# A graph-and-experts kernel on one core: the turning of slot rows and the flag moved one tile back, one batch of statistics split, and GpSimd made to wait for a comparison

## The chip, the cores and the metric

The kernel runs on 1 core of one Trainium2 chip. The metric is device time in microseconds (us). Before the change the median of 3 runs is 608.58 us (606.66 to 609.39). The profile is of one execution.

## The reference

Two layers over 2,500 nodes of 512 features and 80,000 edges sorted by target:

```
edge_index = stack([src, dst])
x = x + gnn(layernorm(x), edge_index)      # h = x + segment_sum(x[src], dst); relu(h @ W1 + b1) @ W2 + b2
x = x + ffn(layernorm(x))                  # softmax gate, top 2 of 8 experts, gelu(x W1[e] + b1[e]) W2[e] + b2[e]
```

The change lies wholly in the first part of the graph layer.

## The kernel before, in words

Each engine has its own written-out order of instructions, and semaphores (`S["..."]`) tie the orders together. The nodes are cut into 20 tiles of 125 rows. `segment_sum` is moved behind the first matrix: z = layernorm(x) W1 is computed for each tile, and the edges are turned into a matrix of counts, 125 "windows" of 20 target nodes each; the counts are then multiplied with z in five groups of 25 windows.

The first 120 us hold two strands of work that share the engines.

**The tiles.** For tile t, ScalarE makes the normed rows (`normal_rows`, tile `xn`), TensorE turns them (`turn_normal`, issued inside `first_layer(t-1)`), ScalarE takes them out of PSUM as float16 (`normal_columns`, `xT_top`), VectorE takes the remainder (`low_columns`, `xT_rest`), and TensorE makes three products of eight matmuls each (`first_layer(t)`: top by high weights, then the turn of tile t+1, then top by low weights, then remainder by high weights). ScalarE writes `z_hi` and `z` (`split_z`), and GpSimd subtracts them (`low_parts`, tile `z_lo`). The means and deviations come from VectorE in batches of tiles (`statistics(b)`, then ScalarE's `roots(b)`, then VectorE's `scales(b)`): batch 4 is tiles 10 to 14, batch 5 tiles 15 to 19. The rows of x for batch 4 are loaded by the queue of SyncE, those of batch 5 by that of ScalarE, once tile 9 has been normed.

**The edges.** VectorE makes keys of the edges (`edge_keys`), SyncE writes them to memory as `edge_pairs`, and GpSimd gathers from there four pieces of slots per window by indirect DMA (`slot_rows`). VectorE compares each edge with the next one and the 255th next (`compare_edges(0)`, `compare_edges(1)`): that tells whether the edges are in order and none is too crowded. `close_rows` puts the nodes' own edges into the gathered rows and sums the flaws. TensorE adds the flaws over partitions (`flaw_sum`), VectorE makes the flag of it (`flag_i`), and the flag goes through memory into `range_row`, from where all engines read it and branch; with these inputs the branch is not taken. TensorE turns the slot rows (`turn_rows`, two parts of four steps, each step two transposes), VectorE takes them (`take_rows(0)` to `take_rows(7)`, two instructions each). Only then can VectorE make the one-hot tables of a window (`one_hots(w)`: `hot_key`, `hot_lo`) and TensorE multiply them (`window(w)`).

TensorE's order is written with two constants:

```
for t in range(FLAG_AT + 1):
    first_layer(t)
    ...
    if t == ROWS_AT:
        flaw_sum()
        turn_rows(0, ROWS_FIRST)
    if t == ROWS_AT + 1:
        turn_rows(ROWS_FIRST, SL)
```

Behind it stand the reading of the flag and the other tiles, each with the windows `counted(t - 1)` to `counted(t)`, where `counted(t)` is 25 * max(t - FLAG_AT, 0) // (19 - FLAG_AT). With ROWS_AT 5 and FLAG_AT 7 tiles 8 to 18 have two windows each and tile 19 three. VectorE's order for this stretch stands in lines 1069 to 1092, and is written by hand in the same way.

Of the kernel before, what the change touches and what calls it, by code (L numbers as in the profile page):

```python
# [16 lines left out]
ALU = mybir.AluOpType  # L17
# [6 lines left out]
KC = D // 128  # L24
# [7 lines left out]
NS = 4  # L32
# [30 lines left out]
HALF = T // 4  # L63
BATCHES = ((0, 2), (2, 4), (4, 6), (6, 10), (10, 15), (15, 20))
ZF = 4
ROWS_AT, FLAG_AT, ROWS_FIRST = 5, 7, 4
GATE_UP = 11
HALVES = (slice(0, DH), slice(DH, DE))
CUTS = (slice(0, 112), slice(112, P))
# [8 lines left out]
def gnn_moe(nc, x, src, dst, gW1, gb1, gW2, gb2, Wg, eW1, eb1, eW2, eb2, out):  # L78
    ctx = ExitStack()
    with ctx:  # L80
# [60 lines left out]
        dst_next = allocator(gather)("dst_next", [P, 2, CPP * CH], I32)  # L141
# [44 lines left out]
        dst_i = sb("dst_i", [P, CPP * CH], I32)  # L186
        src_i = sb("src_i", [P, CPP * CH], I32)
        edge_a = sb("edge_a", [P, CPP, CH], F32)
# [55 lines left out]
        for e in range(NE):  # L244
# [84 lines left out]

        names = (  # L330

            "dst_in src_in next_in x_in_a x_in_b x_in_c x_in_d x_in_e x_in_f ident_ready spans_wide spans_spread w1_in late_in tables keys_ready sources_ready "
            "rows_out chunks_known bounds_gathered starts_known gathered rows_turned rows_used w1_abs_ready w1_second_half w1_summed w1_inverse_ready w1_scaled first_hi_ready first_lo_ready w1_turned w1_scale_ready wg_in wg_abs_ready wg_summed gate_weights gate_x_ready gate_out gate_back gate_parts w2_turned w2_T_ready gate_folded gate_hi_ready "
            "stats_ready std_ready rstd_ready xn_ready xn_turned xn_T_ready xn_low_ready z_done z_hi_ready z_ready z_lo_ready "
            "w2_hi_ready w_split rows_closed flaws_done range_ready range_out range_in bounds_step bounds_ready bounds_out bounds_in "
# [12 lines left out]
        S = {n: sem(n) for n in names}  # L348
# [31 lines left out]
        def load_rows(eng, b):  # L380
            a, end = BATCHES[b]
            place = a % (2 * HALF)
            for cut in CUTS:
                eng.dma_start(x_in[cut, place:place + end - a], x_tiles[cut, a:end]).then_inc(x_in_sems[b], 16)

        @block.sync
        def _(sp):
# [11 lines left out]
            for n, ahead in enumerate((1, FULL)):  # L399
# [1 line left out]
                  .then_inc(S["next_in"], 16)  # L401
                sp.dma_start(dst_next[P - 1:P, n, 0:row - ahead], dst[ahead + (P - 1) * row:E].rearrange("(o e) -> o e", o=1))\
                  .then_inc(S["next_in"], 16)
            sp.wait_ge(S["keys_ready"], 1)
            for cut in CUTS:
                sp.dma_start(edge_pairs[0:E, :].rearrange("(p e) a -> p (e a)", p=P)[cut],
                             pairs_sb[cut].rearrange("p e a -> p (e a)")).then_inc(S["rows_out"], 16)
            sp.wait_ge(S["xn_ready"], HALF)
            load_rows(sp, 4)

            sp.wait_ge(S["range_ready"], 2)
# [117 lines left out]
        def _(pool):  # L529
            step = stepper(pool, S["pool_step"])  # L530
# [48 lines left out]
            def low_parts(a, b):  # L579

                for t in range(a, b):
                    pool.wait_ge(S["z_ready"], t + 1)
                    pool.wait_ge(S["z_hi_ready"], t + 1)
                    pool.tensor_tensor(z_lo[:, t], z[:, t % ZF], z_hi[:, t], ALU.subtract).then_inc(S["z_lo_ready"], 1)  # L584
# [9 lines left out]
            for a in range(NS):  # L594
                pool.indirect_dma_start(out=slot_rows[:, a].rearrange("w e a -> w (e a)"), out_offset=None, in_=edge_pairs[:, :],
                                        in_offset=bass.IndirectOffsetOnAxis(ap=start_i[:, a:a + 1], axis=0)).then_inc(S["gathered"], 16)
            low_parts(2, T)

            for k in range(KC):
                pool.wait_ge(S["w2_hi_ready"], k + 1)  # L600
                ins = pool.tensor_tensor(W2_lo[:, k, 0:D], W2_raw[:, k], W2_hi[:, k, 0:D].bitcast(F32), ALU.subtract)
# [327 lines left out]
        def _(dve):  # L929
            step = stepper(dve, S["dve_step"])  # L930
# [17 lines left out]
            def edge_keys():  # L948
                dve.wait_ge(S["sources_ready"], 1)
                step(dve.scalar_tensor_tensor(edge_a[:].rearrange("p c e -> p (c e)"), lo_part, -float(T), src_i[:], ALU.mult, ALU.add))  # L950
                dve.scalar_tensor_tensor(key_part, dst_i[:], float(T), edge_a[:].rearrange("p c e -> p (c e)"), ALU.mult, ALU.add)\
                   .then_inc(S["keys_ready"], 1)

            def statistics(b):
                a, end = BATCHES[b]
                for t in range(a, end):
                    dve.wait_ge(x_in_sems[b], 32)
                    ins = dve.bn_stats(stat1[:, t], x_in[:, t % (2 * HALF)])  # L958
                step(ins)
                for t in range(a, end):  # L960
                    ins = dve.bn_aggr(mv1[:, t], stat1[:, t])
                ins.then_inc(S["stats_ready"], 1)

            def scales(b):
                a, end = BATCHES[b]
                dve.wait_ge(S["std_ready"], b + 1)
                step(dve.reciprocal(rstd1[:, a:end], std1[:, a:end]))
                dve.scalar_tensor_tensor(shift1[:, a:end], mv1[:, a:end, 0], -1.0, rstd1[:, a:end], ALU.mult, ALU.mult)\
                   .then_inc(S["rstd_ready"], 1)
# [14 lines left out]
            def low_columns(t):  # L984
                dve.wait_ge(S["xn_T_ready"], t + 1)
                if t >= 2:
                    dve.wait_ge(S["z_done"], t - 1)
                dve.tensor_tensor(xT_rest[:, t % 2], psum[:, SM + t % 2, 0:KC * P], xT_top[:, t % 2], ALU.subtract).then_inc(S["xn_low_ready"], 1)
# [28 lines left out]

            def compare_edges(n):
                dve.wait_ge(S["next_in"], 64)
                step(dve.tensor_tensor(edge_a[:].rearrange("p c e -> p (c e)"), dst_i[:], dst_next[:, n], (ALU.is_gt, ALU.is_equal)[n]))  # L1020
                step(dve.tensor_reduce(flaw[:, NS + n:NS + n + 1], edge_a[:], AX.XY, ALU.max))

            def find_starts(a, end):
# [8 lines left out]
            def close_rows():  # L1032
                dve.wait_ge(S["gathered"], 16 * NS)
                step(dve.tensor_tensor(flaw[:, 0:NS], slot_rows[:, :, REAL, 0], key_end[:], ALU.is_lt))
                dve.tensor_copy(slot_rows[:, :, REAL:SLOTS], self_pairs[:]).then_inc(S["rows_closed"], 1)
                step(dve.tensor_reduce(flaw[:, NS + 2:NS + 3], flaw[:, 0:NS + 2], AX.X, ALU.add))
                dve.tensor_copy(flaw[:, 0:1], flaw[:, NS + 2:NS + 3]).then_inc(S["rows_closed"], 1)
# [35 lines left out]
            compare_edges(0)  # L1073
            low_columns(5)
            compare_edges(1)
            close_rows()
            low_columns(6)
            dve.wait_ge(S["flaws_done"], 1)
            dve.tensor_scalar(flag_i[:], psum[0:1, WIN, 510:511], 1.0, None, ALU.min).then_inc(S["range_ready"], 2)
            dve.wait_ge(S["tables"], 3)  # L1080
            for k in range(SL):
                dve.wait_ge(S["rows_turned"], ROWS_FIRST if k < ROWS_FIRST else SL)
                take_rows(k)
                if k == 3:
                    low_columns(7)
            dve.wait_ge(S["rows_used"], SL)
            low_columns(8)
            statistics(4)
            scales(4)

            dve.wait_ge(S["range_in"], 16)
            flag = dve.value_load(range_row[0:1, 2 * NW:], min_val=0, max_val=1)
            with dve.If(flag > 0):
# [19 lines left out]
                for n, (table, j) in enumerate((table, j) for table in (key_all, lo_all) for j in range(CPP)):  # L1113
                    place = table[:, 0:NCH].rearrange("p (c j) -> p j c", j=CPP)[:, j]
# [4 lines left out]
                with dve.Fori(0, NW) as w:  # L1119
                    start = dve.value_load(range_row[0:1, bass.ds(w * 2, 1)], min_val=0, max_val=NCH)  # L1120
                    end = dve.value_load(range_row[0:1, bass.ds(w * 2 + 1, 1)], min_val=1, max_val=NCH + 1)
                    with dve.Fori(start, end) as c:
                        n = dve.snap(visit, min_val=0, max_val=NW * NCH)
# [96 lines left out]
            for it in range(1, G + 1):  # L1220
                g = it - 2
                for j in range(WG):
# [10 lines left out]
                    n = up_slot(it, j, 4) if it < G else None  # L1233
                    if n is not None and n < NE:
                        up_scales(n)
                    n = up_slot(it, j, 7) if it < G else None
# [21 lines left out]
            for c in range(2):  # L1258
                ins = dve.tensor_tensor(chosen[:, c], experts, topf[:, c].rearrange("p (n o) -> p n o", o=1).broadcast_to([P, T, NE]),
                                        ALU.is_equal)  # L1260
# [20 lines left out]
            for c in range(2):  # L1281
                ins = dve.tensor_tensor(picked[:, c], chosen[:, c], slot_of[:].rearrange("p e n -> p n e"), ALU.mult)
# [119 lines left out]
        def _(pe):  # L1402
# [4 lines left out]
            for k in range(KC):  # L1407
                ins = mm(psum[:, WIN + 1, 0:NE], ones[:].broadcast_to([128, 128]), Wg_sb[:, k], start=(k == 0), stop=(k == KC - 1))
# [36 lines left out]
            def first_layer(t):  # L1445
                pe.wait_ge(S["xn_T_ready"], t + 1)
                if t == 0:
                    pe.wait_ge(S["first_hi_ready"], KC)
                    pe.wait_ge(S["gate_weights"], 1)
                if t == 1:  # L1450
                    pe.wait_ge(S["chunks_known"], 1)
                if t >= 2:
                    pe.wait_ge(S["z_ready"], t - 1)
                trio = ((xT_top, W1_hi), (xT_top, W1_lo), (xT_rest, W1_hi))
                for n, (x_, w_) in enumerate(trio):
                    if n == 1 and t < T - 1:
                        turn_normal(t + 1)
                    if n == 1 and t == 0:
                        pe.wait_ge(S["first_lo_ready"], KC)
                    if n == 2:  # L1460
                        pe.wait_ge(S["xn_low_ready"], t + 1)
                    for k in range(KC):
                        for b, columns in enumerate(HALVES):
                            ins = mm(psum[0:P, AGG + 2 * (t % 2) + b, 0:columns.stop - columns.start], x_[:, t % 2, k * P:(k + 1) * P],  # L1464
                                     w_[:, k, columns], start=(n == 0 and k == 0), stop=(n == 2 and k == KC - 1))
                ins.then_inc(S["z_done"], 1)

            def flaw_sum():
# [214 lines left out]
            start = 0  # L1683
# [53 lines left out]
```

## Time and profile before

| what | value |
|---|---|
| median of 3 runs | 608.58 us |
| the profiled execution, its own time | 607.48 us |
| its span | 605.7 us |
| TensorE busy | 530.2 us, 88% |
| VectorE busy | 457.4 us, 76% |
| ScalarE busy | 281.3 us, 46% |
| GpSimd busy | 282.8 us, 47% |
| chain that ended last, by engine | PE 62%, DVE 25%, issue 4%, DMA 3%, ACT 3% |
| mean granted clock of TensorE | 0.947 |

The names in the rows are PE for TensorE's matmuls, DVE for VectorE, ACT for ScalarE, POOL for GpSimd and SP for SyncE; a q behind one is the queue that issues its DMAs. Times count from the start of the span. A row's bracket tells how long the engine was idle ahead of it, and what ended that. The granted clock is a share of 2.4 GHz.

### The profile page before, as it was taken

What the parts mean: (1) busy time and instruction counts of PE and PEld (TensorE: products, weight loads), DVE (VectorE), ACT (ScalarE), POOL (GpSimd) and SP (SyncE); (2) the same over time, 40 slices, a digit from 0 to 9 for tenths busy, and PEclk for the clock granted to TensorE, in tenths of its full rate; (3) what the DMA queues carried; (4) which work ended last, traced back from release to release, by engine and by line L of the source; (5) the groups of instructions that cost most, each with busy time, mean ns of one, the idle gap of its engine ahead of it and who ended that gap; (6) DMA issues with size and microseconds to landing.
All of it is one profiled execution on the core that took longest, in us unless ns stands there. A gap on an engine that the chain in (4) does not pass through costs nothing.

```text
span 605.7 us, 13929 instructions
## 1 busy us (share of the span) xinstructions
PE 530.2 (88%) x4754; PEld 400.2 (66%) x4755; DVE 457.4 (76%) x982; ACT 281.3 (46%) x539; POOL 282.8 (47%) x240
## 2 busy tenths in 40 slices
PE   5968789899989998999999999982489999999980
PEld 3758789657556665666666666571478888888860
DVE  4997678976579999999989334189799676767672
ACT  3763578543153244325432500354367655656561
POOL 7461133221064246324533542531557777778753
PEclk9998799999899999999999999985699999999995
DMA  8363300200050433133322122693698988888875
GB/s 259 134 154 123 85 1 2 79 4 2 2 138 36 136 124 121 69 105 122 121 87 87 54 83 70 174 373 112 200 294 160 163 155 152 161 151 160 147 104 69
DMA packets 40061, 72.25 MB, mean 119 GB/s; under 512 B 12526, under 2 KB 16756, under 8 KB 39338
## 3 DMA queue, kind: packets, MB, share of 16 engines
q0 software_dynamic: 11840, 26.06, 23.7%
q1 hardware_dynamic: 21327, 31.08, 16.3%
q10 hardware_dynamic: 6834, 14.34, 7.3%
q8 instruction: 34, 0.56, 0.4%
q14 instruction: 26, 0.21, 0.1%
HBM read 43.97 MB, written 29.06 MB: 121 GB/s over the span
## 4 chain that ended last, share of the span: by engine, by line
PE 62%; DVE 25%; issue 4%; DMA 3%; ACT 3%; POOL 1%; POOLq 0%; DVEq 0%; SPq 0%; PEldq 0%; ACTq 0%
PE psum L1549 19%; PE psum L1703 10%; PE psum L1693 10%; PE psum L1588 7%; DVE hot_lo L1143 5%; PE psum L1464 5%; PE psum L1533 5%; DVE hot_key L1143 4%; PE psum L1670 3%; DVE stat L958 2%; DMA slot_rows<-edge_pairs,start_i 1%; DMA dst_i<-in_dst 1%; DVE ln L1168 1%; DVE x L1166 1%; ACT h L758 1%
## 5 line engine op out<-in xcount | busy, mean ns | idle before, releaser
L731 ACT ACTIVATE counts<-psum 128x400 bf16<-128x400 f32 x125 | 61.4, 506 | 125.3 <-PE psum L1533 125.3
L1549 PE MATMUL psum<-counts,z_hi 125*128 125x500 bf16 x400 | 102.1, 376 | 2.8 <-ACT h L758 1.9
L1549 PE MATMUL psum<-counts,z_lo 125*128 125x500 bf16 x400 | 101.3, 376 | 0.0
L1143 DVE TENSOR_TENSOR hot_lo<-iota_lo,lo_w 128x1024 f16<-128x1024 f16 x125 | 100.8, 806 | 0.0
L1143 DVE TENSOR_TENSOR hot_key<-iota_key,key_w 128x800 f16<-128x800 f16 x125 | 79.5, 636 | 24.8 <-PE psum L1533 23.5
L670 POOL DMA_INDIRECT out_x<-y,target_i x47 | 75.2, 1600 | 36.7 <-issue 17.9
L1533 PEld LDWEIGHTS psum<-hot_key,hot_lo 128*128 128x128 f16 x1000 | 55.6, 97 | 28.1 <-DVE hot_lo L1143 5.5
L632 POOL TENSOR_TENSOR xt<-xt_whole,xt 125x512 f16<-125x512 f32 x20 | 47.8, 2391 | 49.8 <-DVE xt L1183 36.1
L1533 PE MATMUL psum<-hot_key,hot_lo 128*128 128x100 f16 x1000 | 63.4, 208 | 8.3 <-DVE hot_lo L1143 7.3
L1549 PEld LDWEIGHTS psum<-counts,z_lo 125*128 125x128 f16 x400 | 39.3, 98 | 45.8 <-issue 1.1
L917 ACT ACTIVATE he<-psum,eb_col,up_undo 128x128 f32<-128x128 f32 x94 | 42.5, 457 | 55.9 <-PE psum L1693 54.1
L640 POOL TENSOR_TENSOR x_res<-x_res,b_row 125x512 f32<-125x512 f32 x19 | 29.2, 1545 | 82.1 <-DMA x_res<-in_x 82.1
L1693 PE MATMUL psum<-xT_hi,w_both 128*128 128x128 f16 x704 | 64.6, 220 | 0.0
L1693 PEld LDWEIGHTS psum<-xT_hi,w_both 128*128 128x128 f16 x704 | 52.7, 98 | 14.9 <-DVE xT_lo L1349 14.9
L1693 PE MATMUL psum<-xT_lo,w_both 128*128 128x128 f16 x352 | 61.6, 220 | 0.0
L664 POOL DMA_INDIRECT xg<-xt_d,token_i x47 | 47.3, 1006 | 23.4 <-issue 13.7
L1549 PEld LDWEIGHTS psum<-counts,z_hi 125*128 125x128 f16 x400 | 35.3, 98 | 31.0 <-SPq L486 2.3
L584 POOL TENSOR_TENSOR z_lo<-z,z_hi 125x512 f16<-125x512 f32 x20 | 25.6, 1285 | 60.8 <-ACT z L724 60.8
L1388 DVE CAST he_hi<-he 128x128 fp32r<-128x128 f32 x94 | 22.0, 234 | 27.1 <-ACT he L917 23.2
L1398 DVE SCALAR_TENSOR_TENSOR y<-psum,slot_score,y 128x512 f32<-128x512 f32 x47 | 35.2, 749 | 9.1 <-PE psum L1703 8.8
L1588 PE MATMUL psum<-W_hi,h_hi 128*125 128x264 f32 (+1 forms) x128 | 37.8, 296 | 4.7 <-DVE up_inverse L1190 4.6
L1703 PE MATMUL psum<-w_hi,he_hi 128*128 128x512 f32 x88 | 39.3, 446 | 2.6 <-DVE he_hi L1388 2.5
(274 smaller groups left out, 1125.7 us busy)
## 6 DMA issues: line engine op xcount, KB each, us to landing
out_x<-x SPq DMA_DIRECT2D x20, 224.0 KB
xt_d<-xt SPq DMA_DIRECT2D x20, 224.0 KB
x_res<-in_x SPq DMA_DIRECT2D x19, 224.0 KB
up_raw<-in_L_ffn_W ACTq DMA_DIRECT2D x8, 512.0 KB, 4.0
up_d<-up_split ACTq DMA_DIRECT2D x8, 512.0 KB
w_both<-up_d SPq DMA_DIRECT2D x8, 512.0 KB, 8.0
w_raw<-in_L_ffn_W SPq DMA_DIRECT2D x8, 512.0 KB, 10.0
W_raw<-in_L_gnn_W ACTq DMA_DIRECT2D x2, 1024.0 KB, 5.5
```

The costliest lines, as they stand in the source:

```text
L632: pool.tensor_tensor(xt[:, q, 1], xt_whole[:, n % 2], xt[:, q, 0], ALU.subtract).then_inc(S["xt_ready"], 1)
L664: pool.indirect_dma_start(out=xg[:, k % XB].rearrange("p a d -> p (a d)"), out_offset=None, in_=xt_d[:, :], in_offset=bass.IndirectOffsetO ...
L670: pool.indirect_dma_start(out=out[:, :], in_=y[:, k % YB], in_offset=None, out_offset=bass.IndirectOffsetOnAxis(ap=target_i[:, k:k + 1], a ...
L731: act.activation(counts[:, it % 2, :, place:place + W], psum[:, WIN + w % 2, 0:MW].rearrange("p (w h) -> p h w", w=W), ACT.Copy).then_inc( ...
L917: act.activation(he[:, m], psum[:, 2 + m, 0:B], ACT.Gelu, bias=eb1_col[:, at], scale=up_undo[:, at]).then_inc(S["gelu_ready"], 1)
L1143: ins = dve.tensor_tensor(hot[:, w % RING].rearrange("p s (n two) -> p s n two", two=2), iota[:].rearrange("p (o n two) -> p o n two", o=1 ...
L1398: dve.scalar_tensor_tensor(y[:, k % YB], psum[:, 4], slot_score[:, k:k + 1], y[:, k % YB], ALU.mult, ALU.add).then_inc(S["y_taken"], 1)
L1533: ins = mm(psum[:, WIN + w % 2, a * MH:(a + 1) * MH], hot_lo[:, w % RING, k], hot_key[:, w % RING, k], start=(k == 0), stop=(k == SL - 1))
L1549: ins = mm(psum[:, AGG + c, 0:GN], half[:, t, c * 128:(c + 1) * 128], counts[0:P, g % 2, t], start=(t == 0 and n == 0), stop=(t == T - 1 a ...
L1588: ins = mm(psum[0:P, bank + b, 0:columns.stop - columns.start], h_[:, k, rows], w_[:, k, columns], start=(k == 0 and n == 0), stop=(k == K ...
L1693: ins = mm(psum[:, 2 + m, 0:B], w1_both[e][:, half, c, cols], x_[:, c], start=(c == 0 and i == 0), stop=(c == KC - 1 and i == 2))
L1703: ins = mm(psum[:, 4], h_[:, m], w_[e][:, m], start=(m == 0 and n == 0), stop=(m == HC - 1 and n == 2))
```

## The change

`ROWS_AT` and `FLAG_AT` go up by one, so that tile 6 is put ahead of the sum of flaws and the first turn of slot rows, and tile 8 ahead of the reading of the flag; `counted` then gives tiles 9 to 19 the windows 2, 2, 2, 3, 2, 2, 2, 3, 2, 2, 3. VectorE's order is changed to suit, with statistics and scales of batch 4 put between the takings of rows. GpSimd's `low_parts(2, T)` waits for the second comparison. SyncE's load of batch 4 waits for the four gathers. `first_layer` goes through the four blocks of weights in the order 2, 3, 0, 1, and at tile 0 waits for each block and not for all.

```diff
-ROWS_AT, FLAG_AT, ROWS_FIRST = 5, 7, 4
+ROWS_AT, FLAG_AT, ROWS_FIRST = 6, 8, 4
...
             sp.wait_ge(S["xn_ready"], HALF)
+            sp.wait_ge(S["gathered"], 16 * NS)
             load_rows(sp, 4)
...
                                         in_offset=bass.IndirectOffsetOnAxis(ap=start_i[:, a:a + 1], axis=0)).then_inc(S["gathered"], 16)
+            pool.wait_ge(S["edges_ready"], 2)
             low_parts(2, T)
...
-                step(dve.tensor_tensor(edge_a[:].rearrange("p c e -> p (c e)"), dst_i[:], dst_next[:, n], (ALU.is_gt, ALU.is_equal)[n]))
+                ins = dve.tensor_tensor(edge_a[:].rearrange("p c e -> p (c e)"), dst_i[:], dst_next[:, n], (ALU.is_gt, ALU.is_equal)[n])
+                if n == 0:
+                    step(ins)
+                else:
+                    ins.then_inc(S["edges_ready"], 1)
+                    dve.wait_ge(S["edges_ready"], 2)
...
             compare_edges(1)
+            low_columns(6)
             close_rows()
-            low_columns(6)
+            low_columns(7)
...
                 if k == 3:
-                    low_columns(7)
+                    low_columns(8)
+                    statistics(4)
+                if k == 5:
+                    scales(4)
             dve.wait_ge(S["rows_used"], SL)
-            low_columns(8)
-            statistics(4)
-            scales(4)
+            low_columns(9)
...
                 if t == 0:
-                    pe.wait_ge(S["first_hi_ready"], KC)
                     pe.wait_ge(S["gate_weights"], 1)
...
-                    for k in range(KC):
+                    for place, k in enumerate((2, 3, 0, 1)):
+                        if n == 0 and t == 0:
+                            pe.wait_ge(S["first_hi_ready"], place + 1)
```

The semaphore `keys_ready` is renamed `edges_ready`; its first count is the keys, as before, its second the second comparison. `start` and `stop` of the matmuls go by `place`.

## Rows read from the trace of the kernel before

**Rows 1.** Timeline of TensorE, 0 to 75 us (start, duration, instructions, idle before):

```profile
18.43 1.07 PE L1464 MATMUL psum<-W_hi,xT_top 128*125 128x256 f16 x8 [0.88 <-DVE W_lo L1005]
...
38.61 1.05 PE L1464 MATMUL psum<-W_hi,xT_rest 128*125 128x256 f16 x8
45.17 0.19 PE L1470 MATMUL psum<-ones,flaw 125*1 125x1 f32 x2 [5.51 <-DVE flaw L1037]
45.87 1.91 PE L1482 MATMUL psum<-ident,slot_rows 125*128 125x125 f32 x8 [0.51 <-issue]
...
51.94 1.12 PE L1482 MATMUL psum<-ident,slot_rows 125*128 125x125 f32 x8
...
62.92 0.54 PE L1533 MATMUL psum<-hot_key,hot_lo 128*128 128x100 f16 x8 [3.59 <-DVE hot_lo L1143]
...
65.60 1.96 PE L1464 MATMUL psum<-W_hi,xT_top 128*125 128x256 f16 x8
...
71.90 1.06 PE L1464 MATMUL psum<-W_hi,xT_top 128*125 128x256 f16 x8
```

**Rows 2.** Windows of one us (PE, PEld, DVE, ACT, POOL busy, granted clock, DMA share, GB/s):

```profile
43.00:44.00 1.00, 0.00 (x0) 0.00 (x0) 0.82 (x1) 0.00 (x0) 0.00 (x0) 0.67 0.20 78
...
66.00:67.00 1.00, 1.00 (x7) 1.00 (x6) 1.00 (x3) 0.34 (x1) 0.00 (x0) 0.50 0.53 90
```

**Rows 3.** Timeline of VectorE, 30 to 140 us:

```profile
35.88 0.82 DVE L1020 TENSOR_TENSOR edge_a<-dst_i,dst_next 125x640 f32<-125x640 int32 x1
...
38.19 4.78 DVE L1020 TENSOR_TENSOR edge_a<-dst_i,dst_next 125x640 f32<-125x640 int32 x1
...
44.48 0.16 DVE L1034 TENSOR_TENSOR flaw<-slot_rows,key_end 125x4 f32<-125x4 f32 x1 [0.66 <-DMA slot_rows<-edge_pairs,start_i]
...
44.96 0.15 DVE L1037 COPY flaw<-flaw 125x1 f32<-125x1 f32 x1
...
45.63 0.14 DVE L1079 TENSOR_SCALAR flag_i<-psum 1x1 int32<-1x1 f32 x1
...
53.09 0.42 DVE L1044 TENSOR_TENSOR key_w<-psum,win_base 128x250 f16<-128x250 f32 x1 [1.43 <-PE psum L1482]
...
55.82 0.68 DVE L988 TENSOR_TENSOR xT_rest<-psum,xT_top 128x500 f16<-128x500 f32 x1
56.42 3.06 DVE L958 BATCH_NORM_STATS2 stat<-x_in 125x6 f32<-125x512 f32 x5
...
60.32 0.19 DVE L967 RECIPROCAL rstd<-std 125x5 f32<-125x5 f32 x1 [0.36 <-ACT std L701]
...
61.68 0.57 DVE L1143 TENSOR_TENSOR hot_key<-iota_key,key_w 128x800 f16<-128x800 f16 x1 [0.98 <-issue]
```

**Rows 4.** Timeline of GpSimd, 0 to 125 us:

```profile
35.99 1.77 POOL L595 DMA_INDIRECT slot_rows<-edge_pairs,start_i  x1 [0.30 <-issue]
37.79 4.49 POOL L584 TENSOR_TENSOR z_lo<-z,z_hi 125x512 f16<-125x512 f32 x4
```

**Rows 5.** Timeline of TensorE, 75 to 135 us:

```profile
75.05 0.88 PE L1533 MATMUL psum<-hot_key,hot_lo 128*128 128x100 f16 x16
75.77 1.06 PE L1464 MATMUL psum<-W_hi,xT_top 128*125 128x256 f16 x8
...
84.75 1.06 PE L1464 MATMUL psum<-W_hi,xT_top 128*125 128x256 f16 x8
```

**Rows 6.** Timeline of SyncE's queue, 0 to 125 us:

```profile
30.84 0.76 SPq L384 DMA_DIRECT2D x_in<-in_x  x2
...
48.96 0.42 SPq L457 DMA_DIRECT2D b_col<-in_L_gnn_b  x1
```

**Rows 7.** Page, DMA issues (the last number is the median from issue to landing):

```profile
xg<-xt_d,token_i POOLq DMA_INDIRECT x47, 4.4
```

**Rows 8.** Timeline of ScalarE, 10 to 125 us:

```profile
40.34 0.60 ACT L724 ACTIVATE z<-psum 125x512 f32<-125x512 f32 x1
...
60.74 0.78 ACTq L384 DMA_DIRECT2D x_in<-in_x  x2
```

More of the change, by code:

```diff
@@ L330, in gnn_moe @@
         names = (
-            "dst_in src_in next_in x_in_a x_in_b x_in_c x_in_d x_in_e x_in_f ident_ready spans_wide spans_spread w1_in late_in tables keys_ready sources_ready "
+            "dst_in src_in next_in x_in_a x_in_b x_in_c x_in_d x_in_e x_in_f ident_ready spans_wide spans_spread w1_in late_in tables edges_ready sources_ready "
             "rows_out chunks_known bounds_gathered starts_known gathered rows_turned rows_used w1_abs_ready w1_second_half w1_summed w1_inverse_ready w1_scaled first_hi_ready first_lo_ready w1_turned w1_scale_ready wg_in wg_abs_ready wg_summed gate_weights gate_x_ready gate_out gate_back gate_parts w2_turned w2_T_ready gate_folded gate_hi_ready "
@@ L403, in _ @@
                   .then_inc(S["next_in"], 16)
-            sp.wait_ge(S["keys_ready"], 1)
+            sp.wait_ge(S["edges_ready"], 1)
             for cut in CUTS:
@@ L951, in edge_keys @@
                 dve.scalar_tensor_tensor(key_part, dst_i[:], float(T), edge_a[:].rearrange("p c e -> p (c e)"), ALU.mult, ALU.add)\
-                   .then_inc(S["keys_ready"], 1)
+                   .then_inc(S["edges_ready"], 1)
             def statistics(b):
@@ L1461, in first_layer @@
                         pe.wait_ge(S["xn_low_ready"], t + 1)
-                    for k in range(KC):
+                    for place, k in enumerate((2, 3, 0, 1)):
+                        if n == 0 and t == 0:
+                            pe.wait_ge(S["first_hi_ready"], place + 1)
                         for b, columns in enumerate(HALVES):
                             ins = mm(psum[0:P, AGG + 2 * (t % 2) + b, 0:columns.stop - columns.start], x_[:, t % 2, k * P:(k + 1) * P],
-                                     w_[:, k, columns], start=(n == 0 and k == 0), stop=(n == 2 and k == KC - 1))
+                                     w_[:, k, columns], start=(n == 0 and place == 0), stop=(n == 2 and place == KC - 1))
                 ins.then_inc(S["z_done"], 1)
```

## The prediction

> **What bounds the kernel now.** I read the chain that ended last first. It runs over TensorE for most of its length, so time is won where TensorE stands still or runs at the low clock. The timeline of TensorE shows two such places ahead of the groups, and the change touches both [rows 1]. The first: `first_layer(5)` starts its last eight matmuls at 38.61 and has issued them by 39.50 (eight take 0.89 us between starts); then TensorE idles 5.51 us, adds the flaws at 45.17 and turns slot rows from 45.87. The granted clock fell within 43 to 44 (mean 0.67 there, [rows 2]), some 3.7 us into the idle time: 2.4 to 1.2 GHz. The eight transposes then took 1.71 us between starts (45.87 to 47.58, where tile 6 begins) against 0.95 for the eight at 51.94. The second: idle 3.59 us ahead of window 0 at 62.92, and tile 9 begins at 65.60 with eight matmuls at 1.96 us where those at 71.90 take 1.06, and the clock is 0.50 still in 66 to 67 [rows 1, 2].
>
> VectorE's timeline tells why [rows 3]. The second comparison took 4.78 us from 38.19, the first, of the same shape, 0.82 us. GpSimd's four `z_lo` ran from 37.79 to 42.28 without a gap [rows 4], and 42.28 plus 0.7 is where the comparison ends. Then it waits for the gathers (44.4), closes the rows, and the flag is known at 45.8. The second gap is VectorE's too: between the last `take_rows` (55.8) and `one_hots(0)` (61.68) stand a `low_columns`, statistics and scales of batch 4 and the reading of the flag. In steady state a tile with two windows takes 3.87 us (71.90 to 75.77), of which the windows are 0.72 and `first_layer` 3.15 [rows 1, 5].
>
> **How I sum.** I follow both kernels to one event, the start of `first_layer(10)`. Before: 71.90, with four windows done. After: two windows done, so it owes 0.72 us of TensorE.
>
> **The order of blocks at tile 0.** Tile 0 begins at 18.43, released by the gate's low weights (VectorE, L1005) [rows 1]. That wait stays. Worth 0; at most 0.1, since the wait for the four blocks was not the last. Another order of blocks in the same eight matmuls costs nothing.
>
> **GpSimd waits.** The comparison starts at 38.19 as before and takes 0.85 us with nothing of GpSimd's in its way; `z_lo` starts at 39.1 in place of 37.79. Behind the wait stand the `z_lo` of all tiles; who waits for them is ScalarE's `z`, four tiles later, and it has slack of several us. VectorE reduces until 39.9 and does `low_columns(6)` until 40.5.
>
> **Tile 6 in the gap.** TensorE has tile 6's columns by then (its turn is in `first_layer(5)`), so `first_layer(6)` runs 39.50 to 42.65; its third product, due 41.8, finds `low_columns(6)` done. This hides 3.15 us of the 5.51.
>
> **Closing the rows.** The gathers landed at 44.4 with the 1.25 MB load of batch 4 issued at 30.84, just ahead of them [rows 3, 6]. Now that load waits for them. The last gather is issued at 35.99 [rows 4]; a gather of equal size (128 rows of 2 KB) lands 4.4 us after issue later in this kernel [rows 7], which would be 40.4. Bounds: 40.4 and 44.4; I take 41 to 43, nearer to the unloaded row. But `close_rows` begins with a comparison of two SBUF operands, the kind that stood still under `z_lo`, and the four `z_lo` now run 39.1 to 43.6 (4.49 us, no gap: tile 5's z was done at 40.94 [rows 8]). So I take 43.6 for its start. The Trainium skill, "SBUF — State Buffer", section "Who interferes with whom", says that a VectorE instruction with two SBUF inputs, or in a two-port copy mode, is shut out for the whole of a GpSimd instruction that reads SBUF and started first; the 4.78 us agrees, and by it the port conflict isn't removed but moved from the comparison to the closing; without the rule the closing would go at the landing.
>
> From the first instruction of closing to the end of its last was 0.65 us (44.48 to 45.11) [rows 3]: 44.25. `low_columns(7)` 0.6, flag 0.15, TensorE released 0.24 us after it started (45.63 to 45.87): turns begin at 45.1, not 45.87. TensorE stood still for 2.4 us, less than the 3.7 after which it fell before, so I take the high clock and 0.95 us for the turns.
>
> **VectorE's chain from there.** First `take_rows` 1.15 us after the turns begin (51.94 to 53.09): 46.25. Four takings are 2.7 us (53.09 to 55.82), `low_columns(8)` 0.6, statistics 3.5 (56.42 to 59.96, where ScalarE's root is waited for), two takings 1.35, scales 0.4, two takings 1.35, `low_columns(9)` 0.6, flag 1.0 (the idle 0.98 ahead of 61.68) [rows 3]: 11.5 in all, 57.75. ScalarE's root is now under two takings, which wins 0.36. Two windows of tables at 1.1 us each: 59.95; I add 0.45 for a `z_lo` that meets one of them, as between 0 and 1.1 (one `z_lo`). The last window's matmuls 0.36: `first_layer(10)` at **60.75**.
>
> TensorE by itself would need 46.05 + three tiles + 0.95 + two windows, 57.2: it is 3.5 us ahead of VectorE, so VectorE's chain sets the event, and TensorE's short waits (for the norm of tile 10, behind scales, about 1 us in tile 9) cost nothing.
>
> **The moved load.** Batch 4 is issued when the gathers land, 41 to 44.4. Batch 5, of equal size, was issued at 60.74 and the last bytes moved in 66 to 67: 5.8 us [rows 2, 8]. So it lands at 47 to 50.2; statistics want it at 49.55. Cost 0 to 0.7, taken 0. Behind it in SyncE's queue go the flag's two hops, which before were over 3.2 us after the flag (48.96, [rows 6]); behind the load they end by 54 at the latest. TensorE wants the flag at 53.3 and has slack, VectorE at 56.75: 0.
>
> **Later.** Tile 12 has three windows in place of two, right behind statistics of batch 5. There VectorE is the slower: 75.77 to 84.75 is 1.24 us over two periods [rows 5]. One more window costs 1.1 us on VectorE against 0.36 on TensorE: 0.73 lost. In tile 16 VectorE's third table is ready a us before TensorE asks, so 0. From the groups on nothing changes, and the gain is carried to the end.
>
> **Sum.** 71.90 - 60.75 - 0.72 - 0.73 = 9.7 us. The profiled execution: 607.48 - 9.7 = 597.8; the median stood 1.1 us over it, so 598.9, written 599.
>
> **Rivals.**
>
> *Late closing, low clock* (20%). The gathers land at 44.4 as before. Tile 6's z is then done at about 44.1 (42.65 plus what tile 5 took from 39.50 to 40.94), and its `z_lo` holds the port to 45.3: closing begins there, 1.7 us later. TensorE stands still for 4.1 us, over the 3.7, and the clock falls: the first turns cost 0.76 more. `first_layer(7)` is 2 us slower under the slack of 3.5. Gain 9.7 - 2.5 = 7.2: 601.4. For it: nothing here shows a gather of this place without the load. The Trainium skill, "TensorE: Matmul & The Clock Gate", also has the clock fall for idle time; this trace shows it twice.
>
> *No collision* (13%). The gathers land by 41.5 and closing slips in; turns follow tile 6 at 42.65, 2.45 us earlier. Gain 12.1: 596.5. Against it: the comparison found no gap in four `z_lo`.
>
> *The comparison stays slow* (7%): the change doesn't do what it says, because something other than `z_lo` held it. It ends at 42.97, `z_lo` runs to 47.5, closing then: 3.9 us later and a low clock, 0.76. Gain 5.0: 603.6. Against it: the end of the stall fits to 0.1 us.
>
> *Statistics starve the windows* (5%, the one that ends slower). They stand between takings, so if batch 4's rows are late, all behind them is late us for us. Due at 49.55: landed at 59.3 there is no gain, at 62.3 the kernel is 0.5% slower, 612. That would be about 18 us after issue, against 5.8. Half of this case reaches either point.
>
> **Chances and range.** Forecast (gain 8.5 to 10.8) 55%, rivals as above. The forecast's own spread is 1.2 for the blocked last copy of closing (tile 6's `z_lo` may start just ahead of it) and 0.45 for the meeting in the tables. The range takes the no-collision case at one end and the slow comparison at the other: 596 to 603.6. Half a percent, 3.0 us, is about what a measurement can tell: faster 0.93, same 0.04, slower 0.03.
>
> **What would show it.** Right: second comparison 0.8 us; `z_lo` x4 from 39.1; `first_layer(6)` at 39.5; gathers landed by 43; L1034 at about 43.6; turns at 45.1 at full clock; first `hot_key` at 57.8; `first_layer(10)` at 60.8; the start of the groups (L1549) 9.7 us earlier than before. Wrong: L1034 behind a landing at 44.4, a granted clock of 0.5 after 45, VectorE idle ahead of its `BATCH_NORM_STATS2` of batch 4, or the groups giving time back.

## The result and the profile after

The changed kernel takes 604.75 us (median of 14 runs, 601.49 to 607.19), the kernel before on the same chip 608.38 (606.66 to 610.5): ratio 0.9937, 95% interval 0.9922 to 0.9953. It is faster, by some 3.8 us, where 9.7 was forecast. The profiled execution took 604.76 us.

The page of the changed kernel: its span, and the granted clock in 40 slices.

```profile
span 603.0 us, 13929 instructions
...
PEclk9999799899999999999999999985699999999995
```

VectorE's timeline of the changed kernel answers to [rows 3]:

```profile
38.63 0.81 DVE L1022 TENSOR_TENSOR edge_a<-dst_i,dst_next 125x640 f32<-125x640 int32 x1
...
42.22 0.72 DVE L1041 TENSOR_TENSOR flaw<-slot_rows,key_end 125x4 f32<-125x4 f32 x1 [1.21 <-DMA slot_rows<-edge_pairs,start_i]
42.97 1.10 DVE L1042 COPY slot_rows<-self_pairs 125x40 f32<-125x40 f32 x1
...
44.17 0.15 DVE L1044 COPY flaw<-flaw 125x1 f32<-125x1 f32 x1
...
49.92 3.07 DVE L960 BATCH_NORM_STATS2 stat<-x_in 125x6 f32<-125x512 f32 x5 [0.25 <-DMA x_in<-in_x]
...
57.52 0.58 DVE L1152 TENSOR_TENSOR hot_key<-iota_key,key_w 128x800 f16<-128x800 f16 x1 [0.47 <-issue]
...
62.34 0.68 DVE L990 TENSOR_TENSOR xT_rest<-psum,xT_top 128x500 f16<-128x500 f32 x1 [2.55 <-ACT xT_top L716]
```

and GpSimd's to [rows 4]:

```profile
39.53 4.50 POOL L585 TENSOR_TENSOR z_lo<-z,z_hi 125x512 f16<-125x512 f32 x4 [1.32 <-DVE edge_a L1022]
```

The second comparison takes 0.81 us, the gathers have landed by 42.2, and the closing of the rows meets the `z_lo`: its first two instructions need 0.72 and 1.10 us in place of 0.16 and 0.18. So the closing starts at 42.22, where 43.6 was forecast, but it ends at 44.3, as forecast (44.25). The first tables come at 57.52, forecast 57.75. Up to here no event that the sum runs over is off by more than 0.5 us. Then, on VectorE too, comes a wait that the forecast didn't have, of 2.55 us. TensorE's timeline, which answers to [rows 1, 5]:

```profile
39.94 1.05 PE L1474 MATMUL psum<-W_hi,xT_top 128*125 128x256 f16 x8
...
44.38 0.19 PE L1480 MATMUL psum<-ones,flaw 125*1 125x1 f32 x2 [1.14 <-DVE flaw L1044]
45.09 1.20 PE L1492 MATMUL psum<-ident,slot_rows 125*128 125x125 f32 x8 [0.52 <-issue]
46.12 1.05 PE L1474 MATMUL psum<-W_hi,xT_top 128*125 128x256 f16 x8
...
58.76 0.53 PE L1543 MATMUL psum<-hot_key,hot_lo 128*128 128x100 f16 x8 [0.30 <-DVE hot_lo L1152]
...
62.36 1.99 PE L1474 MATMUL psum<-W_hi,xT_top 128*125 128x256 f16 x8 [1.98 <-ACT xT_top L716]
...
68.95 1.06 PE L1474 MATMUL psum<-W_hi,xT_top 128*125 128x256 f16 x8
...
72.83 1.06 PE L1474 MATMUL psum<-W_hi,xT_top 128*125 128x256 f16 x8
...
79.02 1.06 PE L1474 MATMUL psum<-W_hi,xT_top 128*125 128x256 f16 x8
...
92.21 1.06 PE L1474 MATMUL psum<-W_hi,xT_top 128*125 128x256 f16 x8
...
97.25 0.53 PE L1543 MATMUL psum<-hot_key,hot_lo 128*128 128x100 f16 x8 [1.01 <-ACT counts L733]
97.62 1.06 PE L1474 MATMUL psum<-W_hi,xT_top 128*125 128x256 f16 x8
...
111.76 1.29 PE L1559 MATMUL psum<-counts,z_hi 125*128 125x500 bf16 x4 [0.90 <-SPq L487]
112.85 1.87 PE L1559 MATMUL psum<-counts,z_lo 125*128 125x500 bf16 x4
```

The turns begin at 45.09 (forecast 45.1) and at the full clock: eight of them and tile 7 follow in 1.03 us. The loss stands at 62.36: `first_layer(10)` waits 1.98 us for ScalarE, and its matmuls then run at the low clock (1.99 us for eight, not 1.06). ScalarE's timeline tells what it was doing, SyncE's queue what stood ahead of it; these answer to [rows 8] and [rows 6]:

```profile
55.08 0.81 ACT L709 ACTIVATE xn<-x_in,shift,rstd 125x512 f32<-125x512 f32 x1 [1.27 <-DVE shift L970]
55.08 5.46 ACTq L384 DMA_DIRECT2D x_in<-in_x  x2
60.59 0.60 ACT L722 ACTIVATE z_hi<-psum 125x512 f16<-125x512 f32 x1 [4.70 <-issue]
```

```profile
42.26 0.76 SPq L384 DMA_DIRECT2D x_in<-in_x  x2
...
53.37 0.67 SPq L461 DMA_DIRECT2D out_x<-in_x  x1
```

To issue the two DMAs of batch 5's load ScalarE needs 5.46 us, against 0.78 before. It is an engine like the others: while its queue can't get a DMA out, `z_hi` of tile 8 waits, and so the columns of tile 10. SyncE had started to issue a copy of 1.5 MB (the 768 spare rows, line 461) 1.7 us before; before the change there were 10.4 us between the two starts. Of the two DMAs the first goes out in 0.33 us, and the second is the one that is held, for 5.10 us.

### The profile page after: what moved, and what is told of

Same layout as the page of the kernel before. It is cut to its first block, busy times and chain, and to the rows that moved or that the text cites. A ratio compares the mean times of both kernels' runs of the same rounds, so it can differ in the third digit from the quotient of the medians.

```text
span 603.0 us, 13929 instructions
## 1 busy us (share of the span) xinstructions
PE 530.9 (88%) x4754; PEld 399.1 (66%) x4755; DVE 457.4 (76%) x982; ACT 281.1 (47%) x539; POOL 283.7 (47%) x240
## 4 chain that ended last, share of the span: by engine, by line
PE 61%; DVE 23%; DMA 5%; issue 4%; ACT 4%; ACTq 1%; POOL 1%; POOLq 0%; SPq 0%; DVEq 0%; PEldq 0%
PE psum L1559 20%; PE psum L1713 10%; PE psum L1703 10%; PE psum L1598 7%; DVE hot_lo L1152 5%; PE psum L1543 5%; PE psum L1474 4%; DVE hot_key L1152 4%; PE psum L1680 3%; DMA bound_rows<-in_dst,chunk_i 2%; DVE stat L960 1%; DMA x_in<-in_x 1%; DMA dst_i<-in_dst 1%; DVE ln L1177 1%; DVE x L1175 1%
```

## The experiments

**Without the copy.**

```diff
-            sp.dma_start(out[N:N + PAD, :], x[0:PAD, :]).then_inc(S["spare_out"], 16)
...
             for it in range(G + 1):
+                if it == 1:
+                    sp.dma_start(out[N:N + PAD, :], x[0:PAD, :]).then_inc(S["spare_out"], 16)
```

> The changed kernel, with SyncE's copy of the 768 spare rows (1.5 MB, memory to memory, in the changed kernel issued at 53.4 us) moved behind the first group of counts. Theory A (the gain was lost because ScalarE's issue of batch 5's load stood behind that copy for 5.46 us): the two issues take 0.8 us, first_layer(10) begins at 60.2 to 60.8 in place of 62.4 and at the full clock, so that first_layer(11) begins 4 to 5 us earlier than in the changed kernel (64.2 against 68.95); the kernel is 4 to 5 us faster than the changed one, ratio to before about 0.986. Rival B (the issue is slow for some other reason, such as the small loads just ahead of it, and the low clock would come anyway): the issue stays at 5 us and the ratio at 0.994.

Measured: ratio 0.9874 (0.9852 to 0.9897), some 4 us faster than the changed kernel. ScalarE's timeline:

```profile
55.63 1.14 ACTq L384 DMA_DIRECT2D x_in<-in_x  x2
```

The hold is gone, as theory A has it. But `first_layer(10)` began at 62.69, no earlier: in this execution the clock fell at the turns, though TensorE had been idle as long as in the changed kernel:

```profile
44.41 0.19 PE L1481 MATMUL psum<-ones,flaw 125*1 125x1 f32 x2 [1.15 <-DVE flaw L1045]
45.11 1.60 PE L1493 MATMUL psum<-ident,slot_rows 125*128 125x125 f32 x8 [0.51 <-issue]
46.50 1.94 PE L1475 MATMUL psum<-W_hi,xT_top 128*125 128x256 f16 x8
```

So two things are mixed here, and the clock needs a run of its own. The same run shows a hold without the copy in flight and without ScalarE's queue being the one that waits. SyncE's issue of the 1.5 MB copy came at 111 us, 1.3 us after ScalarE's load of the second matrix (1 MB), and took 6.15 us in place of 0.67. ScalarE's queue, then SyncE's:

```profile
109.73 0.40 ACTq L827 DMA_DIRECT2D W_raw<-in_L_gnn_W  x1
```

```profile
111.03 6.15 SPq L467 DMA_DIRECT2D out_x<-in_x  x1
```

**The copy just ahead of the load, in the kernel before.**

```diff
+            sp.wait_ge(S["stats_ready"], 5)
             sp.dma_start(out[N:N + PAD, :], x[0:PAD, :]).then_inc(S["spare_out"], 16)
```

> The kernel before, with the same copy held until the statistics of batch 4 are done (about 60.0 us), so that it goes out just ahead of ScalarE's load of batch 5 (60.7). Theory A: ScalarE's two issues, 0.78 us before, take 4 to 6 us, z of tile 8 and the columns of tile 10 come as much later, and the kernel is 3 to 5 us slower than before (ratio 1.005 to 1.008). Rival B: the issues stay under 1 us and the ratio at 1.000.

Measured: ratio 1.0011 (0.9992 to 1.003). SyncE's queue, then ScalarE's:

```profile
61.32 0.67 SPq L461 DMA_DIRECT2D out_x<-in_x  x1
```

```profile
62.08 0.78 ACTq L384 DMA_DIRECT2D x_in<-in_x  x2
```

A miss. An issue 0.76 us after the copy's isn't held. Theory A in the form "an issue behind the copy is held" falls.

**The load issued by SyncE.** `load_rows(act, 5)` is taken out of ScalarE's order, and SyncE gets, behind the copy:

```diff
+            sp.wait_ge(S["xn_ready"], 2 * HALF)
+            load_rows(sp, 5)
```

> The changed kernel, with the copy left in its place and batch 5's load issued by SyncE's queue behind it, not by ScalarE's. Theory A (only the engine that issues is held, the transfer itself is in time): SyncE's issue takes some 5 us and hurts nobody, ScalarE goes on at 55.9, the gain is that of the late copy, ratio about 0.986, unless the rows land after 71.7, when statistics of batch 5 want them. Rival B (the copy slows ScalarE's or TensorE's own work through memory): ScalarE is late by the same 5 us with no DMA of its own, ratio 0.994.

Measured: ratio 0.9871 (0.9845 to 0.9897). SyncE's queue:

```profile
54.15 3.31 SPq L384 DMA_DIRECT2D x_in<-in_x  x2
```

SyncE is held for 3.31 us and hurts nobody; ScalarE isn't late, `first_layer(10)` begins at 61.31 at the full clock, the groups at 108.03, 8.0 us before the kernel before reaches them (116.01 there) and 3.7 us before the changed one (111.76). The transfer was in time. This is theory A against its rival: what costs is the engine that issues, not the transfer. (This execution is 0.6 us later at the turns than that of the changed kernel, 45.72, so 61.31 is near the forecast's 60.75.)

**Batch 4's load without its wait.**

```diff
             sp.wait_ge(S["xn_ready"], HALF)
-            sp.wait_ge(S["gathered"], 16 * NS)
             load_rows(sp, 4)
```

> The changed kernel without SyncE's wait for the gathers: batch 4 is loaded from about 31 us, as before the change. If the load is what slowed the gathers: they land at 44.4 again and not by 42.2, the closing of rows waits for them and for the z_lo of tile 6, the turns begin near 46.5 with a low clock likely, and first tables come 1.5 to 2.5 us later than at 57.5; but flag and copy go out some 4 us earlier too, so the issue of batch 5 should be short, and the ratio could even be better than 0.994. If the gathers land by 42.2 without the wait, it was worth nothing.

Measured: ratio 0.9913 (0.9882 to 0.9944). VectorE's timeline:

```profile
44.73 0.82 DVE L1040 TENSOR_TENSOR flaw<-slot_rows,key_end 125x4 f32<-125x4 f32 x1 [3.93 <-DMA slot_rows<-edge_pairs,start_i]
```

The gathers land 2.5 us later, the closing also meets the `z_lo` of tile 6 (0.82 for 0.16), turns begin at 46.78, the clock falls a us later, the first tables come at 59.31. That was the rival "late closing, low clock", and it costs 1.8 us at the tables, not 2.5. ScalarE's issue, 5.6 us after the copy's, still took 3.52. In time this run can't be told from the changed kernel: the two intervals overlap.

**The small loads away, the copy in place.** The three loads of biases ahead of the copy (lines 458 to 460) go behind the first group.

```diff
-            sp.dma_start(b1_col[:], gb1.rearrange("(k p) -> p k", p=128), allow_slow_non_contiguous=True).then_inc(S["late_in"], 16)
...
+                if it == 1:
+                    sp.dma_start(b1_col[:], gb1.rearrange("(k p) -> p k", p=128), allow_slow_non_contiguous=True).then_inc(S["late_in"], 16)
```

> The changed kernel with the copy in its place (about 52 us now, right behind the flag's second hop) and the three small loads of the biases (two columns of 4-byte elements, one row for all partitions) moved behind the first group of counts. Theory A1 (what holds ScalarE's issue is a queue filled by the small loads and the copy together): the issue takes under 1.5 us. Rival A2 (the copy alone holds it, once it has been running for more than about a us: the copy was only 0.8 us ahead in the run where it didn't hold): the issue takes 3 to 5 us still, a little less for the copy's earlier start.

**The copy further ahead, in the kernel before.**

```diff
+            sp.wait_ge(S["xn_T_ready"], 9)
             sp.dma_start(out[N:N + PAD, :], x[0:PAD, :]).then_inc(S["spare_out"], 16)
```

> The kernel before with the copy held until the columns of tile 8 are out (about 58.2 us), 2.5 us ahead of ScalarE's load of batch 5 at 60.7, the small loads done long before. Theory A1: the issue takes 0.8 us, time as before. Rival A2: the issue takes 4 to 6 us, z of tile 8 and the columns of tile 10 come as much later; VectorE's windows 0 and 1 go on, and the kernel is 2 to 4 us slower than before (ratio 1.003 to 1.007).

Measured, ScalarE's issue in the first and the second:

```profile
54.89 2.72 ACTq L384 DMA_DIRECT2D x_in<-in_x  x2
```

```profile
60.23 1.44 ACTq L384 DMA_DIRECT2D x_in<-in_x  x2
```

Ratios 0.989 (0.9851 to 0.993) and 0.9974 (0.9953 to 0.9996). Without the small loads the issue is held for less, yet held: neither A1's 1.5 us nor A2's 3 to 5. In the second the copy went out at 54.56, earlier than I had meant, 5.7 us ahead; the hold was short and the kernel no slower. All profiled executions in which ScalarE issues the load, in us:

| run | small loads | from the copy's issue to ScalarE's | ScalarE's issue took | copy landed after |
|---|---|---|---|---|
| copy just ahead, in the kernel before | long before the copy | 0.8 | 0.78 | 8.1 |
| changed kernel once more | just ahead of the copy | 1.6 | 5.34 | 10.1 |
| changed kernel | just ahead | 1.7 | 5.46 | 10.1 |
| small loads away | none | 3.8 | 2.72 | 7.1 |
| GpSimd without its wait | just ahead | 4.0 | 5.53 | 10.6 |
| batch 4 without its wait | just ahead | 5.6 | 3.52 | 9.4 |
| copy further ahead, in the kernel before | 4.9 us before the copy | 5.7 | 1.44 | 8.0 |
| the two waits alone | just ahead | 7.5 | 1.45 | 9.1 |
| the kernel before | just ahead | 10.4 | 0.78 | 9.1 |
| without the copy | 3.1 us before the load | no copy | 1.14 | |

An issue that came 1.6 to 7.5 us after the copy's was held, and got out 0.2 to 3.1 us before the copy had landed; one that came 0.8 us after it, or after the landing, was not. At like distances the hold was shorter where the small loads didn't stand just ahead of the copy. What in the queues is full was not seen.

**Extra windows elsewhere.** With SyncE's load; `counted` gives tiles 14, 18 and 19 three windows, and the first of the three in 14 and 18 goes ahead of the tile.

```diff
+                if leads(t):
+                    window(counted(t - 1))
                 first_layer(t)
-                for w in range(counted(t - 1), counted(t)):
+                for w in range(counted(t - 1) + leads(t), counted(t)):
```

> The changed kernel with batch 5's load issued by SyncE's queue, and with the extra windows in tiles 14, 18 and 19 in place of 12, 16 and 19, the first of the three in tiles 14 and 18 put ahead of the tile. If a third window costs what the timeline shows (tile 12 behind the statistics, and a wait for ScalarE's counts of 1.0 us in tile 16 since only two banks hold windows), tiles with three windows take 4.2 us in place of 5.4, and the groups begin 1.5 to 2 us earlier than with the issue moved alone (106.3 against 108.0); ratio about 0.984. If the wait for counts only moves, they begin at 108 again.

Measured: ratio 0.989 (0.9856 to 0.9924), groups at 108.62. The tiles between 92.89 and 98.31 show why: 5.42 us, as in tile 16 of the changed kernel. A window ahead of tile 18 comes right behind the two of tile 17, and three in a row is what has to wait. (The row of the third names VectorE as its releaser, but that window's own table was ready at 96.85, 1.1 us before it ran.) The wait only moved. In tile 14 it also met VectorE behind batch 5's statistics: 7.5 us from one tile to the next.

**GpSimd without its wait.**

```diff
-            pool.wait_ge(S["edges_ready"], 2)
             low_parts(2, T)
```

> The changed kernel without GpSimd's wait for the second comparison. If the port conflict was what held the comparison: it takes 4.8 us again, low_columns(6) comes at 44, first_layer(6) ends at 45, closing follows at once (the gathers having landed at 42), turns begin at 46 against 45.1, and the first tables come about 1 us later than at 57.5. Ratio 0.994 to 0.997. If not, the comparison takes 0.8 us as it stands.

Measured: ratio 0.9937 (0.9905 to 0.9969). VectorE, then GpSimd:

```profile
38.20 4.79 DVE L1021 TENSOR_TENSOR edge_a<-dst_i,dst_next 125x640 f32<-125x640 int32 x1
...
44.47 0.15 DVE L1040 TENSOR_TENSOR flaw<-slot_rows,key_end 125x4 f32<-125x4 f32 x1
```

```profile
37.78 4.50 POOL L585 TENSOR_TENSOR z_lo<-z,z_hi 125x512 f16<-125x512 f32 x4
```

The comparison takes 4.79 us again: the port conflict is shown. Turns at 46.18, tables at 59.12, 1.6 us late. Yet the kernel's time can't be told from that of the changed one. The groups begin at 112.03, 0.3 us later: ScalarE is held until 62.2 in place of 60.5, but tile 10 took 5.2 us, not 6.6, its low stretch being shorter. The waits ahead of 60 us are drowned by what comes behind them.

**The changed kernel once more.**

> The changed kernel itself once more. Two low stretches of its clock come where TensorE had hardly been idle: 61 to 68 us and 112 to 116 us. Theory C (the clock's falls are not fixed by the program: the same gap can cost a low stretch or not): some of the low stretches at 45, 61, 112 and 150 us come or go with all starts before them the same to 0.5 us, and the span differs by 1.6 us for each. Rival D: the same stretches, the same span.

Measured: 601.7 us, span 599.9. ScalarE's issue and TensorE's rows:

```profile
54.78 5.34 ACTq L384 DMA_DIRECT2D x_in<-in_x  x2
```

```profile
61.94 1.99 PE L1474 MATMUL psum<-W_hi,xT_top 128*125 128x256 f16 x8 [1.86 <-ACT xT_top L716]
...
64.56 1.24 PE L1474 MATMUL psum<-W_lo,xT_top 128*125 128x256 f16 x8
```

The hold is there again, 5.34 us: it belongs to the program. The clock doesn't: the low stretch ends at 65, not at 68, and there is none at the groups, so the spans differ by 3.1 us. Of it, 0.4 lay ahead of tile 10, 1.3 was tile 10 (61.94 to 67.24 is 5.30 us, 6.59 in the first) and 1.65 the start of the groups (62.87 us from there to the first matmul of the second matrix, 64.52 in the first), together 3.4, near the 3.1. Theory C, from two executions; with one timed run this says nothing of the median.

**Windows inside the tiles.** With SyncE's load; `counted` gives tiles 16, 18 and 19 three windows, and the first of the three goes between the second and third product:

```diff
                     if n == 2:
+                        if between(t):
+                            window(counted(t - 1))
                         pe.wait_ge(S["xn_low_ready"], t + 1)
```

> The changed kernel with batch 5's load issued by SyncE's queue, and the extra windows in tiles 16, 18 and 19, each put inside its tile (between its second and third product), so that no three windows follow each other. If a third window costs a wait for ScalarE's counts (1.0 us) because three in a row meet two banks: tiles 16, 18 and 19 take 4.25 us in place of 5.4, tile 12 to 13 takes 5.1, and the groups begin 2.7 us before those of the run with the load moved alone (105.3 against 108.0). Low stretches of the clock aside, ratio 0.983.

Measured: ratio 0.9845 (0.9822 to 0.9867), the smallest of all, and its interval lies clear of the changed kernel's: this version beats the kernel before and the changed one. From the run with SyncE's load alone (0.9845 to 0.9897) the time doesn't tell it apart; the timeline does. Tiles 16 and 18 take 4.25 and 4.24 us. Tile 12, with two windows behind the statistics, takes 5.5, not 5.1. The groups begin at 106.92, not 105.3, for the last two windows now wait for VectorE:

```profile
104.30 0.52 PE L1549 MATMUL psum<-hot_key,hot_lo 128*128 128x100 f16 x8 [0.57 <-DVE hot_lo L1156]
106.36 0.77 PE L1549 MATMUL psum<-hot_key,hot_lo 128*128 128x100 f16 x8 [1.54 <-DVE hot_lo L1156]
```

**And TensorE kept busy.** The same, with 20 matmuls whose sums nobody reads.

```diff
+            def keep_busy(t, n):
+                for _ in range(n):
+                    mm(psum[:, SM + t % 2, 0:MW], self_row[:, 0:128], self_cols[:], start=True, stop=True)
...
                 if t == ROWS_AT:
+                    keep_busy(t, 8)
                     flaw_sum()
```

> The same, and TensorE given 20 idle matmuls of 400 columns (their sums read by nobody): 8 ahead of the sum of flaws, 3 ahead of window 0, 5 ahead of the groups, 4 within the folding of the gate, where it has forty matmuls of 8 columns. Each takes 0.17 us. Theory C: no low stretch at 45, 61 or 112 us, and a shorter one or none at 145 us; costs 1 us of matmuls, gains 1.6 for each stretch spared: ratio about 0.980. Rival: the clock falls all the same and the kernel is 1 us slower than without them.

Measured: ratio 0.9885 (0.9858 to 0.9912). The profiled execution had a single low stretch ahead of 399 us, 143 to 147, and the shortest span of all profiled executions, 597.6; but the median of the six timed runs is 601.85 (599.35 to 603.5), against 599.69 without the extra matmuls, and the intervals overlap. Whether the matmuls help on average is open; a gain isn't shown.

**The two waits alone.** The kernel before with SyncE's wait for the gathers and GpSimd's for the comparison.

```diff
+            sp.wait_ge(S["gathered"], 16 * NS)
             load_rows(sp, 4)
...
+            pool.wait_ge(S["keys_ready"], 2)
             low_parts(2, T)
```

> The kernel before with only the two waits of the change (batch 4's load behind the gathers, GpSimd behind the second comparison); order of tiles, statistics and flag as before. The comparison takes 0.8 us, the rows land at 42 and are closed at 43 to 44.3, turns begin at 44.5 to 45 in place of 45.9; statistics of batch 4 wait for nothing. Gain 1 to 1.5 us: the waits by themselves are the smaller part, the tile in the gap and the statistics under the turns the larger. Ratio 0.998.

Measured: ratio 0.996 (0.9941 to 0.9979). Turns at 45.10, 0.8 us ahead of before, groups at 113.82, 2.2 us ahead, more than expected: tables of window 1 no longer met a `z_lo`, and its matmuls came 1.09 us after window 0's, not 2.04. ScalarE's issue took 1.45 us here. The waits by themselves bring some 2.4 us of the 3.8 that the whole change measured. The intervals of the two overlap by a little, so it is likely, not certain, that the tile in the gap and the statistics under the turns added something on top. With the load on SyncE the whole change gains 7.8 us (ratio 0.9871), 5.4 more than the waits alone: most of what the tile and the statistics could bring was lost again behind the hold.

## Why the prediction was wrong

Right, by the timeline: the port conflict and its end; the gathers landed by 42.2 with the load behind them; the closing done at 44.3 (forecast 44.25); turns at 45.09 (45.1) at the full clock; `take_rows` at 46.39 (46.25); the wait for batch 4's rows 0.25 us (0 to 0.7); tables at 57.52 (57.75); tile 0 at 18.39 (18.43 before), so the other order of blocks was worth nothing; tile 12 to 13 longer by 1.08 us, 0.72 over its window (0.73).

The Trainium skill's port rule ("SBUF — State Buffer", section "Who interferes with whom") held also for what speaks against the change: the closing was shut out in its turn, its copy taking 1.10 us in place of 0.18 beside the fourth `z_lo`. One detail was off: it got in between the third and the fourth `z_lo`, where I had seen no gap.

That the clock stayed up at the turns was luck in part. I compared 2.4 us of standing still with the 3.7 after which the clock had fallen before. With idle times of 1.13 to 1.15 and 0.51 to 0.52 us there, and so some 2 us from the last product to the turns, the granted clock stayed at 1.0 in five profiled executions and fell to 0.5 in two (without the copy, and with the extra windows elsewhere). The rule of the prediction doesn't tell the two apart.

Wrong, by the forecast's steps, in the profiled execution:

| step of the sum | forecast | measured | lost |
|---|---|---|---|
| `first_layer(10)` begins | 60.75 | 62.36 | 1.6 |
| tile 10 at the full clock | 3.87 | 6.59 | 2.7 |
| tile 16, "VectorE's third table is ready a us before TensorE asks, so 0" | 4.23 | 5.41 | 1.2 |
| from the groups to the second matrix, "From the groups on nothing changes" | 62.87 | 64.52 | 1.65 |

Together 7.2, and 9.7 less 7.2 is 2.5; the spans differ by 2.7. The medians differ by 3.8, since the profiled execution of the kernel before was 0.9 us below its median.

**The step that failed first** is "The moved load". I counted what stands behind batch 4's load on SyncE's queue, found that the flag's hops had time, and priced them at 0. I didn't follow the queue one DMA further: the copy behind the flag's hops moved from 50.39 to 53.37, and ScalarE's load, released by the earlier scales, from 60.74 to 55.08. They met. The load taken off ScalarE (same order of everything else) brings tile 10 to the forecast time and the groups 3.7 us earlier than in the changed kernel. That the meeting of the two causes the hold is shown by taking away the copy (1.14 us) and by giving the load to SyncE (3.31 us there, none on ScalarE); the mechanism inside the queues is not.

**The low clock** over tile 10 came behind the hold in the changed kernel: TensorE stood for 1.98 us behind a stretch of two windows and waits; with the load on SyncE there was no low stretch there. It isn't the hold's alone: in the run without the copy tile 10 ran at the low clock too, behind waits of 1.25 and 1.51 us for tables. That the size varies (1.4 or 2.7 us lost on tile 10) is the clock's, not the program's.

**The third window** was compared with the wrong engine. I asked when VectorE's table is ready; the wait was for ScalarE's counts of the window two before, since windows use two banks: 1.01 us. VectorE's third table was indeed ready at 95.4, 0.8 us before TensorE asked. The trace before the change showed this wait, in the one tile that had three windows then, tile 19:

```profile
114.12 0.93 PE L1533 MATMUL psum<-hot_key,hot_lo 128*128 128x100 f16 x16 [1.01 <-ACT counts L731]
```

With the window inside the tile a tile of three takes 4.25 us, as the forecast has it.

**At the groups** the gap is the same before and after (0.96 and 0.90 us, then the first counts), and the clock fell in one of two executions of the same kernel. That loss isn't the change's.

The range failed with it: all rivals were mishaps ahead of 61 us, and none had the program's later DMAs or the clock in it.

## What to carry to other kernels

When a step is moved, follow its queue to the last DMA that shifts, and ask of each big one what another engine will want to issue while it is in flight: a queue that can't issue stops the engine's arithmetic. Give big loads to the engine that computes nothing. And where a kernel has gaps of 1 to 3 us in TensorE's work, two executions can differ by several us through the clock alone, so a forecast from one trace needs that as a term of its range.

## What of the hardware was unexpected

An issue of two DMAs on ScalarE's queue, 0.78 us in the kernel before, took 2.7 to 5.5 us in four programs and 1.4 in two more while SyncE's 1.5 MB copy was in flight, but 0.78 when it came 0.76 us after the copy's issue. It goes the other way round too: in two programs an issue of SyncE's took 6.0 and 6.15 us, 1.3 us after ScalarE's load of 1 MB, while one that came 0.7 us after that load took 0.27.

The clock's low stretches differ between executions: with TensorE idle 1.14 us, 0.52 us and busy around it the clock stayed up in the changed kernel, and fell in the run without the copy, with the same gaps to 0.01 us. In all fourteen profiled executions a low stretch of 3 to 8 us began within the folding of the gate (forty matmuls of 8 columns, 4.4 to 6.0 us long) or up to 0.3 us behind it, while TensorE counted as 100% busy.
